# Group two's squares of a two-layer convolution kernel: half streams made by ScalarE copies and accumulating DMAs instead of VectorE

## What is computed

```python
x = x + _L0_conv_ref(_gn(x), w3, b3, w5, b5, wr, br)   # a 3x3 and a 5x5 convolution, the 3x3 result
                                                       # in nine shifts, mixed by wr
x = x + _L1_conv_ref(_gn(x), filters)                  # filters [32, 32, 10, 10]
```

## Time and profile before

| | before |
|---|---|
| median of 3 runs | 303.13 us (302.38 to 303.31) |
| profiled execution, first to last instruction (span) | 300.4 us |
| profiled execution's own time | not given apart from the span; the median of the runs lies 2.7 us above the span |
| mean granted TensorE clock over the span | 0.986 |
| PE busy | 273.3 us (91%) |
| DVE busy | 252.8 us (84%) |
| ACT busy | 87.6 us (29%) |
| POOL busy | 29.0 us (10%) |

### The profile page before, as it was taken

One profiled execution on the slowest core, in us unless ns is written; L12 is line 12 of the kernel. 1 busy time (PEld: TensorE's weight loads), 2 busy tenths in 40 slices (PEclk: granted clock), 3 DMA queues, 4 the chain that ended last, 5 costly groups with the idle time before them and its releaser, 6 DMA issues.

```text
span 300.4 us, 13567 instructions
## 1 busy us (share of the span) xinstructions
PE 273.3 (91%) x6464; PEld 130.6 (43%) x6464; DVE 252.8 (84%) x216; ACT 87.6 (29%) x135; POOL 29.0 (10%) x82
## 2 busy tenths in 40 slices
PE   0589999899999999999999999999999999999930
PEld 0224343344434433363546475344345446467310
DVE  1899899998999979799999999984999999970330
ACT  4532006979169789539000000004000000000000
POOL 7913920000110000000000000000000000000000
PEclk9999999999999999999999999999999999999995
DMA  6973000000000000000000000085000000000049
GB/s 190 382 203 82 4 2 3 2 5 2 2 2 4 4 2 4 2 2 3 4 2 4 2 4 4 2 171 115 2 2 4 2 2 4 2 4 4 2 91 189
DMA packets 19206, 11.45 MB, mean 38 GB/s; under 512 B 17744, under 2 KB 17872, under 8 KB 19024
## 3 DMA queue, kind: packets, MB, share of 16 engines
q1 hardware_dynamic: 14640, 9.06, 11.9%
q10 hardware_dynamic: 4512, 1.53, 2.2%
HBM read 6.40 MB, written 4.19 MB: 35 GB/s over the span
## 4 chain that ended last, share of the span: by engine, by line
PE 71%; DVE 15%; ACT 4%; issue 3%; DMA 2%; SPq 1%; DVEq 0%
PE acc L1007 63%; PE acc L1050 7%; ACT raw L507 3%; DMA raw<-in_x 2%; DVE stats L741 2%; DVE product L637 2%; DVE plane L759 2%; PE acc L1101 2%; DVE scaled L637 1%; DVE raw L801 1%; DVE product L872 1%; DVE product L663 1%; DVE product L669 1%; DVE arena L669 1%; DVE product L673 1%
## 5 line engine op out<-in xcount | busy, mean ns | idle before, releaser
L1007 PE MATMUL acc<-product,weight 32*32 32x512 f32 (+1 forms) x3072 | 126.8, 604 | 0.3 <-DVE product L872 0.3
L1007 PEld LDWEIGHTS acc<-product,weight 32*32 32x32 f32 (+1 forms) x3072 | 65.2, 110 | 59.4 <-issue 41.5
L879 DVE TENSOR_TENSOR product<-plane 128x4096 f32<-128x4096 f32 x19 | 83.3, 4430 | 0.1
L1007 PE MATMUL acc<-raw,weight 32*32 32x512 f32 (+1 forms) x960 | 45.4, 604 | 0.0
L1050 PE MATMUL acc<-product,middle 32*64 32x512 f32 (+1 forms) x576 | 30.2, 598 | 0.0
L1007 PEld LDWEIGHTS acc<-raw,weight 32*32 32x32 f32 (+1 forms) x960 | 20.7, 112 | 20.2 <-issue 15.7
L801 DVE TENSOR_TENSOR raw<-acc,arena 128x512 f32<-128x512 f32 x16 | 9.9, 683 | 16.7 <-issue 16.6
L1007 PE MATMUL acc<-product,arena 32*32 32x512 f32 (+1 forms) x448 | 22.2, 604 | 0.0
L879 DVE TENSOR_TENSOR raw<-plane 128x4096 f32<-128x4096 f32 x5 | 22.1, 4428 | 0.0
L741 DVE BATCH_NORM_STATS2 stats<-raw 128x6 f32<-128x512 f32 x32 | 19.7, 681 | 2.7 <-DMA raw<-in_x 2.6
L507 ACT ACTIVATE raw<-arena 32x512 f32<-32x512 f32 x32 | 21.8, 681 | 0.5
(11 more groups left out here) (121 smaller groups left out, 209.9 us busy)
## 6 DMA issues: line engine op xcount, KB each, us to landing
raw<-in_x SPq DMA_DIRECT2D x8, 512.0 KB, 8.3
out<-raw SPq DMA_DIRECT2D x24, 128.0 KB, 3.0
arena<-in_L_conv_filters SPq DMA_DIRECT2D x4, 400.0 KB, 6.9
out<-raw ACTq DMA_DIRECT2D x8, 128.0 KB, 4.7
arena<-in_L_conv_w ACTq DMA_DIRECT2D x4, 100.0 KB, 4.0
w_in<-in_L_conv_w ACTq DMA_DIRECT2D x2, 36.0 KB, 1.8
w_in<-in_L_conv_w SPq DMA_DIRECT2D x2, 36.0 KB, 2.2
b_in<-in_L_conv_b SPq DMA_DIRECT2D x2, 0.5 KB
```

The costliest lines, as they stand in the source:

```text
L879: nc.vector.tensor_tensor(both_halves(g, u), plane_halves(g), plane_halves(g, PRODUCTS[k][0] * PITCH + PRODUCTS[k][1]), ALU.mult)\
L1007: return nc.tensor.matmul(acc[32 * s:32 * (s + strips), j, r, :], weights[32 * r:32 * r + 32, t:t + strips, :] .rearrange("p t c -> p (t c ...
```

## The change

The four DVE instructions on group two's squares are taken out. In their place ACT writes one of the two operands into the destination (a copy, with scale -1 where it is subtracted), and POOL issues a DMA that adds the other operand onto it. The transfers run over whole rows with their gap column, 64 x 33 elements per partition, in runs of at most 4,224 bytes. Square left and right get a new home, `spare`, a buffer that takes in the conv zero taps (`scaled3`, `weight0`, `middle0` and others), from element 2081 on, behind `kept_cross`; square sum and cross go to group one's `plane[0]`, once DVE has made group one's last unit from it. `NEXT_SIDES` moves its wait from `SQUARE_MIXED` of its own group to unit 15 of group one, and unit 8's wait stays on `LINEAR`. DVE waits for all four additions before unit 7, which overwrites `SQUARE`; PE waits for each of them where it waited for a count of `stream_made`.

```diff
+SPARE_AT = GROUP * CHUNK + HPITCH
+SPARE_LEN = 206 * C
...
-             {LINEAR: 0, SQUARE: "raw1", SQUARE_MIXED: 1, NEXT: 2, LINEAR_SIDES: 3, SQUARE_SIDES: 0, NEXT_SIDES: 1,
+             {LINEAR: 0, SQUARE: "raw1", SQUARE_MIXED: "plane0", NEXT: 2, LINEAR_SIDES: 3, SQUARE_SIDES: "spare",
+              NEXT_SIDES: 1,
...
-        ["linear sum", "linear cross", "square sum", "square cross", "next", "linear left", "linear right",
-         "square left", "square right", "next left", "next right"] + list(range(7, LAST_UNIT + 1)))
+        ["linear sum", "linear cross", "next", "linear left", "linear right", "next left", "next right"] + list(range(7, LAST_UNIT + 1)))
...
-        scaled3 = sb("scaled3", [128, len(EY_EX), 9, C])
+        spare = sb("spare", [128, SPARE_LEN])
...
+        scaled3 = early(9 * len(EY_EX)).rearrange("p (n t c) -> p n t c", t=9, c=C)
...
-        weight0 = sb("weight0", [128, N_WEIGHT0, C])
+        weight0 = early(N_WEIGHT0).rearrange("p (n c) -> p n c", c=C)
...
+        def half_run(g, u, half, shift=0):
+            tile, at = home(g, u)
+            return view(tile, at + half * HALF_LEN + HALF_AT + shift, (1, H * HPITCH))
...
             stream_borders(raw[1]).then_inc(borders, 1)
+            pool.wait_ge(edges_done, 2 * NG)
+            stream_borders(spare, SPARE_AT).then_inc(borders, 1)
+            def add_square(n, name, u, half, other, shift):
+                pool.wait_ge(square_put, n)
+                pool.dma_start(half_run(1, u, half), half_run(1, SQUARE, other, shift), accum_op=ALU.add,
+                               max_dma_last_dim=H // 2 * HPITCH * 4)\
+                    .then_inc(square_added[name], 16)
+            add_square(1, "left", SQUARE_SIDES, 0, 1, -1)
+            add_square(2, "right", SQUARE_SIDES, 1, 0, 1)
+            pool.wait_ge(stream_made, made(0, LAST_UNIT))
+            stream_borders(plane[0]).then_inc(borders, 1)
+            add_square(3, "sum", SQUARE_MIXED, 0, 1, 0)
+            add_square(4, "cross", SQUARE_MIXED, 1, 1, 0)
...
+            def put_square_sides():
+                act.wait_ge(square_ready, NG)
+                act.wait_ge(borders, 7)
+                for half in (0, 1):
+                    nc.scalar.activation(half_stream(1, SQUARE_SIDES, half), half_stream(1, SQUARE, 1 - half),
+                                         ACT.Copy, scale=-1.0).then_inc(square_put, 1)
+            def put_square_mixed():
+                act.wait_ge(borders, 8)
+                for half, sign in ((0, 1.0), (1, -1.0)):
+                    nc.scalar.activation(half_stream(1, SQUARE_MIXED, half), half_stream(1, SQUARE, 0),
+                                         ACT.Copy, scale=sign).then_inc(square_put, 1)
...
             square(1)
+            put_square_sides()
+            put_square_mixed()
             keep_sum(1)
...
-                elif u in (LINEAR, SQUARE_MIXED, NEXT, LINEAR_SIDES):
-                    wait_used(dve, 0, {LINEAR: 13, SQUARE_MIXED: 15, NEXT: 16, LINEAR_SIDES: 17}[u])
+                elif u in (LINEAR, NEXT_SIDES, NEXT, LINEAR_SIDES):
+                    wait_used(dve, 0, {LINEAR: 13, NEXT_SIDES: 15, NEXT: 16, LINEAR_SIDES: 17}[u])
...
-                    before = {SQUARE_SIDES: LINEAR, NEXT_SIDES: SQUARE_MIXED, 8: LINEAR, 9: LINEAR_SIDES,
-                              10: SQUARE_SIDES, 11: NEXT_SIDES, 12: 7, 13: 8, 14: 9, 15: 10, 16: 11, 17: 12}.get(u)
+                    before = {8: LINEAR, 9: LINEAR_SIDES, 10: LINEAR, 11: NEXT_SIDES, 12: 7, 13: 8, 14: 9, 15: 10, 16: 11, 17: 12}.get(u)
...
+                if u == 7 and g == 1:
+                    for name in square_added:
+                        dve.wait_ge(square_added[name], 16)
...
             linear_cross(1)
-            square_sum(1)
-            square_cross(1)
             evict(0, 0)
             multiply(1, NEXT)
             evict(0, 1)
             linear_left(1)
             linear_right(1)
-            square_left(1)
-            square_right(1)
             next_left(1)
...
+                if g == 1 and name == "square":
+                    pe.wait_ge(square_added[sum_or_cross], 16)
```

More of the change, by code:

```diff
@@ L124, in conv_kernel, with early @@
         filters_in = arena[:, 0:FILTER_LEN]
-        w3_in = sb("w3_in", [128, C * 9])
-        w3_taps = sb("w3_taps", [128, 9, C])
-        scaled3 = sb("scaled3", [128, len(EY_EX), 9, C])
+        spare = sb("spare", [128, SPARE_LEN])
+        spare_used = [0]
+        def early(n):
+            at = spare_used[0]
+            spare_used[0] += n * C
+            return spare[:, at:at + n * C]
+        scaled3 = early(9 * len(EY_EX)).rearrange("p (n t c) -> p n t c", t=9, c=C)
+        w3_in = early(9)
+        w3_taps = early(9).rearrange("p (t c) -> p t c", c=C)
         at = FILTER_LEN
@@ L136, in conv_kernel @@
         w5_taps = arena[:, at + C * 25:at + 2 * C * 25].rearrange("p (n c) -> p n c", c=C)
-        weight0 = sb("weight0", [128, N_WEIGHT0, C])
+        weight0 = early(N_WEIGHT0).rearrange("p (n c) -> p n c", c=C)
         weight1 = sb("weight1", [128, N_WEIGHT1, C])
[L140 to L143, removed]
+        middle0 = [early(15).rearrange("p (k t c) -> p k t c", t=5, c=C) for g in range(NG)]
+        minus_one, half_one, outer_sum = (early(5).rearrange("p (t c) -> p t c", c=C) for n in range(3))
         small = arena[:, small_at:small_at + 26 * C].rearrange("p (n c) -> p n c", c=C)
@@ L149, in conv_kernel @@
         next_sum = sb("next_sum", [128, 3, C])
-        eye_from = sb("eye_from", [128, 4, C])
-        eye_wide = sb("eye_wide", [128, 4, C])
+        eye_from, eye_wide = (early(4).rearrange("p (j c) -> p j c", c=C) for n in range(2))
         eye = sb("eye", [128, C])
@@ L225, in conv_kernel @@
         unit_used = sem("unit_used")
+        square_put = sem("square_put")
+        square_added = {name: sem(f"square_{name}_added") for name in ("sum", "cross", "left", "right")}
         stored = sem("stored")
@@ L243, in home @@
             place = UNIT_HOME[g][u]
-            return {"raw0": raw[0], "raw1": raw[1]}[place] if isinstance(place, str) else product[place]
+            named = {"raw0": (raw[0], 0), "raw1": (raw[1], 0), "plane0": (plane[0], 0), "spare": (spare, SPARE_AT)}
+            return named[place] if isinstance(place, str) else (product[place], 0)
         def view(tile, at, *dims):
@@ L250, in half_stream @@
         def half_stream(g, u, half, shift=0):
-            return view(home(g, u), half * HALF_LEN + HALF_AT + shift, (HPITCH, H), (1, HALF_W))
+            tile, at = home(g, u)
+            return view(tile, at + half * HALF_LEN + HALF_AT + shift, (HPITCH, H), (1, HALF_W))
+        def half_run(g, u, half, shift=0):
+            tile, at = home(g, u)
+            return view(tile, at + half * HALF_LEN + HALF_AT + shift, (1, H * HPITCH))
         def both_halves(g, u):
-            return view(home(g, u), HALF_AT, (HPITCH, H), (HALF_LEN, 2), (1, HALF_W))
+            tile, at = home(g, u)
+            return view(tile, at + HALF_AT, (HPITCH, H), (HALF_LEN, 2), (1, HALF_W))
         def plane_halves(g, shift=0):
@@ L405, in _ @@
                 nc.gpsimd.tensor_tensor(edge_parts(0, e), edge_parts(0, e),
-                                        view(scaled3, scaled_at(-1, e, 2, 0),
+                                        view(spare, scaled_at(-1, e, 2, 0),
                                              (scaled_at(1, e, 0, 0) - scaled_at(-1, e, 2, 0), 2), (3 * C, 3), (1, C)),
@@ L409, in _ @@
                 nc.gpsimd.tensor_tensor(edge_parts(2, e), edge_parts(2, e),
-                                        view(scaled3, scaled_at(e, 1, 0, 0),
+                                        view(spare, scaled_at(e, 1, 0, 0),
                                              (scaled_at(e, -1, 0, 2) - scaled_at(e, 1, 0, 0), 2), (C, 3), (1, C)),
@@ L416, in _ @@
                 top = scaled_at(-1, ex, 2, 1 - ex)
-                last = nc.gpsimd.tensor_tensor(part, part, view(scaled3, top, (scaled_at(1, ex, 0, 1 - ex) - top, 2),
+                last = nc.gpsimd.tensor_tensor(part, part, view(spare, top, (scaled_at(1, ex, 0, 1 - ex) - top, 2),
                                                                 (1, C)), ALU.add)
@@ L444, in _, with stream_borders @@
             last.then_inc(sums_ready, 1)
[L447 to L450, removed]
+            def stream_borders(tile, at=0):
+                nc.gpsimd.memset(view(tile, at, (HALF_LEN, 2), (1, HALF_AT)), 0.0)
+                nc.gpsimd.memset(view(tile, at + HALF_AT + HALF_W, (HALF_LEN, 2), (HPITCH, H)), 0.0)
+                return nc.gpsimd.memset(view(tile, at + HALF_AT + H * HPITCH, (HALF_LEN, 2), (1, HPITCH)), 0.0)
             pool.wait_ge(part_done, 7)
@@ L842, in wait_free @@
                     dve.wait_ge(borders, {3: 1, 0: 2, 1: 3, "raw0": 4, 2: 5}[UNIT_HOME[g][u]])
-                elif u in (LINEAR, SQUARE_MIXED, NEXT, LINEAR_SIDES):
```

(26 more changed lines are left out.)

## The result

The changed kernel takes **308.16 us** (median of 4 runs, 308.07 to 308.59); the kernel before, run beside it, 303.04 us (302.38 to 303.31). The ratio is 1.0186 with a 95% interval of 1.0158 to 1.0214: slower by 5.1 us, outside the range of the prediction (302.2 to 305.5), and by a mechanism that is none of its rivals.

The account below looks back on a forecast made before the run. PE was taken as the bound, so 9.0 us less DVE work was worth 0 and every added term cost 0: span 300.4 plus 2.7 around it gave 303.1 us, range 302.2 to 305.5.

Parts of the forecast that it names:

- its rivals: Late additions (up to 307.5 us, chance 0.12), DVE held up by POOL's descriptors (305.0 or 307.0, 0.12), DVE the bound (294.1, 0.06).
- PE is the bound, the removed DVE work is worth nothing: Four DVE instructions, 9.0 us in sum, lie off the path: PE's run hides them, worth 0.
- The waits were put at 4.5 and 9.2: DVE idle from 183.3 to 187.8 before the first eviction, and from 214.7 to about 223.9 before unit 9.
- Copies and borders free: Four ACT copies of 2.16 us each and two POOL border sets, one taking 0.49 us: cost 0.
- DVE not held up by POOL's descriptors: POOL's descriptor work beside DVE taken as 0, bounds 0 to 2.0 us an issue; the opposing rival had chance 0.12.
- A launch cost: A first POOL queue at launch: between nothing and part of 2.7 us, taken as 0; over 0.9 us had chance 0.03.
- The prediction's 2.7 us: Time around the span, added to the 300.4 us span to give the 303.1 us median.
- Additions in time for their readers: Additions of 7.5 us each; sum landing at 189.0 and cross at 194.7, before PE wants them at 195.4 and 202.7.
- the lead of 6.4 us: Square sum's addition was to land at 189.0, with PE wanting it at 195.4.
- Added on the DMA queues ... Cost 0: Four additions of 1.08 MB each on a new queue, 7.5 us apiece, hidden before their readers: cost 0.
- the first rival: Late additions: PE stalls at square sum or cross, shown by a gap ended by a DMA; up to 307.5 us, chance 0.12.

Follow-up runs that it names:

- the additions beside pairs: Kernel before plus two idle additions of 1.08 MB, back to back, from about 112 us beside 32 x 64 pairs: 302.66 us, ratio 0.9991.
- the row of six: Kernel before plus six idle additions of 1.08 MB back to back from about 143 us: 311.8 us; each cut into four DMAs: 311.81 us.
- single additions: Changed kernel with right held until group one's unit 14 and cross until its first eviction, so no two additions run back to back: 303.1 us, ratio 1.0006.
- the six copies on SP's queue: Kernel before plus six plain copies of 2.16 MB from SP's hardware queue: 317.29 us, ratio 1.0487.
- copies on POOL's queue: Kernel before plus six plain copies of 2.16 MB from POOL's queue, each issued when the one before has landed: 314.08 us, ratio 1.0345.
- six additions in parts: Kernel before plus six idle additions, each in four DMAs of 0.27 MB, 24 back to back: 311.81 us, ratio 1.0294.

## Why the prediction was wrong

- **PE is the bound, the removed DVE work is worth nothing: right.** The change without its additions equals the kernel before, and what DVE saved turned into waiting. The timeline of DVE, against the earlier trace rows:

```profile
179.82 4.51 DVE L916 TENSOR_TENSOR product<-plane 128x2048 f32<-128x2048 f32 x2
193.48 2.48 DVE L855 TENSOR_TENSOR raw<-acc,arena 128x512 f32<-128x512 f32 x4 [9.15 <-PE acc L1059]
...
215.84 4.42 DVE L935 TENSOR_TENSOR product<-plane 128x4096 f32<-128x4096 f32 x1
230.26 4.48 DVE L935 TENSOR_TENSOR product<-plane 128x4096 f32<-128x4096 f32 x1 [10.00 <-PE acc L1059]
```

  The waits were put at 4.5 and 9.2, and in the run without the additions they are 4.48 and 9.33; here they are longer because PE came late.
- **Copies and borders free: right** (copies 1.86 us each, taken 2.16). **DVE not held up by POOL's descriptors: right.** Issues took 1.20 to 1.33 us. Beside those at 145.70 and 147.49 DVE had no multiply but `mix`, whose two sets of four instructions took 2.73 and 2.74 us (2.74 and 2.74 before); the multiplies behind them kept 4.4 us. A launch cost did not show either: an execution's time is 1.7 to 1.8 us above its own span in the changed kernel and in the kernel before alike. The prediction's 2.7 us set one execution's span against the median of others.
- **Additions in time for their readers: right, their size wrong.** One moves its bytes in 6.0 to 6.6 us; the first of a pair lands 9.6 us after its issue, the second after 12.8 (taken: 7.5 from issue to landing, bounds 4.6 to 14.3). Of the lead of 6.4 us there was enough for this.
- **"Added on the DMA queues ... Cost 0": the step that failed.** It priced the additions for those who wait for them, not for who else uses the DMA engines. Worse, it named the witness: "nothing else on the DMA engines from 182 to 194 (2 to 4 GB/s)". Those 2 to 4 GB/s are 16 KB in 4 to 7 us, PE's program. In place of 0 the step is worth 3.1 us for the pair at 147 and 2.4 for the pair at 184. PE lists no wait of this kind in the profile before, so the first rival looked for a gap ended by a DMA. The gaps came, ended by "issue".

The Trainium skill, page "Runtime: NRT & Kernel Launch", section "Instruction fetch mechanics", says that an engine's instructions arrive in blocks of 16 KiB through a DMA queue of its sequencer's own, while it works on the ones before, and that this is mostly hidden. The prediction did not weigh it. The trace agrees on the size (50 transfers, 0.82 MB) and, before the change, on hidden; behind two pairs of long additions it cost 5.1 us. The Trainium skill, page "SBUF — State Buffer", section "Who interferes with whom", says "DMA never contends with a compute engine". The runs agree for the operands (no cost beside pairs, and the pace inside a block unchanged) but not for the engine as a whole.

The traces also show how far ahead PE fetches. In the kernel before, a fetch starts as PE comes to the end of a block (blocks begin at 113.46, 120.50 and 127.26, fetches at 113.34, 119.62 and 126.68), and it brings the block behind the one that PE then begins: the fetch at 153.20 stands beside the block that begins at 153.70, and its counterpart in the changed kernel, at 159.82, ends the stop before the block after that (162.07). So a fetch has one block's time, 4.4 us in singles or 7.0 in pairs, less the 2.3 from its start to PE's next record: as an estimate, a slack of 2.1 or 4.7 us. That fits the additions beside pairs, where fetches came at 111.55 and 122.33, 10.8 us apart (7.0 + 4.7 = 11.7), without loss.

Three things stay open. The stores of the kernel before keep the DMA engines as full (0.91) in pieces of 256 bytes, against 4,224 in the additions, and its fetches at 199.14 and 204.47 came on time; whether shorter pieces would mend the additions was not tried. Cutting the additions into four took nearly all of the loss from the two pairs (303.51 against 308.16 us) and nothing from the row of six, where a fetch still waited for four or five parts; the runs do not show why. And which DMA engines carry the fetches, and by what turn they get in, no view here shows.

## What to carry to other kernels

A long, unrolled program on TensorE is itself a stream on the DMA engines: read the instruction queue's row and divide its transfers by TensorE's pace. A transfer that nobody waits for can still cost time when it keeps the DMA engines full for much longer than one such block lasts TensorE: here some 12.5 us cost 2 to 3 us beside blocks of 4.0 to 6.0 us and nothing beside blocks of 7.0, and single additions of 6.4 to 7.4 us cost 0.6 in all. So put bulk copies beside slow records or one at a time, with a pause for the fetches between. An "issue" gap in TensorE's chain beside a full DMA window is the sign.

## What was not expected of the hardware

- TensorE, with operands, weights and semaphores all ready, stood for up to 3.1 us beside full DMA engines; copies on SP's hardware queue cost more (14.8 us for six of 2.16 MB) than additions on POOL's (9.2 us for six of 1.08 MB).
- Cutting a DMA into four did not let a fetch in at each boundary: it waited for four or five.
- After such stops the granted clock can fall. The windows of the six copies on SP's queue show means of 0.96 and then 0.83, with PE at the lower level (1.2 GHz) for 3.4 us from 163.4 on, while in the changed kernel it stayed at 1.00 after a stop of 2.14 us. The length of a stop does not tell the cases apart: the clock fell at one of 2.27 us (copies on POOL's queue) and not after one of 2.74 (six additions in parts):

```profile
156.00:164.00 8.00, 4.90 (x148) 2.89 (x128) 8.00 (x3) 0.00 (x0) 0.00 (x0) 0.96 0.72 217
164.00:172.00 8.00, 8.00 (x183) 4.37 (x173) 8.00 (x3) 0.00 (x0) 0.00 (x0) 0.83 0.89 274
```
